# Two weighing steps in a row: pairs of column-tiled matmuls in units 1, 2, 9 and 10

## The chip, the core and the metric

The kernel is one program on one core of a Trainium2 chip. The metric is the device time of the launch in microseconds. A core has five engines that run side by side, each through its own queue and strictly in that queue's order: TensorE (PE, with its weight loads shown apart as PEld), VectorE (DVE), ScalarE (ACT), GpSimd (POOL) and SyncE (SP, which here issues DMAs). They wait for each other by semaphores.

## The reference

Four sequences of 512 tokens, 128 channels wide, go through three layers: a block of attention with rotary positions and a mixture of experts, a plain attention, and the first block again.

```python
def _L0_ffn_ref(src, ...):
    q = (src @ Wq).reshape(Bb, Tt, H, DH).transpose(0, 2, 1, 3)          # 16 heads of 8
    k = (src @ Wk_c @ Wk).reshape(Bb, Tt, H, DH).transpose(0, 2, 1, 3)
    v = (src @ Wv_c @ Wv).reshape(Bb, Tt, H, DH).transpose(0, 2, 1, 3)
    q, k = _apply_rope(q, sin, cos), _apply_rope(k, sin, cos)
    attn = jax.nn.softmax(jnp.einsum('bhqd,bhkd->bhqk', q, k) / np.sqrt(DH), axis=-1)
    sa = jnp.einsum('bhqk,bhkd->bhqd', attn, v).transpose(0, 2, 1, 3).reshape(Bb, Tt, C) @ Wo
    x = _rmsnorm(src + sa, norm1_w)
    shared = _swiglu(flat @ W_shared_in) @ W_shared_out
    ...                                   # a gate picks 2 of 8 experts, weights w
    h = _swiglu(flat @ W1_shared)
    for e in range(E):
        routed = routed + h @ W2_experts[e] * w[:, e:e + 1]
    return _rmsnorm(x + (shared + routed).reshape(Bb, Tt, C), norm2_w)

x = x + 0.5 * _L0_ffn_ref(_layernorm(x), ...)
x = x + _L0_attn_ref(_layernorm(x), ...)                                  # 16 heads of 4
x = x + 0.5 * _L0_ffn_ref(_layernorm(x), ...)
```

## The kernel before, in words

A unit is one sequence in one layer: units 0 to 3 and 8 to 11 are of the block with experts, 4 to 7 of the plain attention. What a unit does is cut into named steps, and `plan()` writes all steps of all units into one list. Each engine walks the same list and does its own share of each step. So the list is the order of the work on every engine.

The list is built from places. A unit has 64 places, and in each stands one tile of scores that goes into the softmax (`exp_scores`: a 128x512 matmul of keys and queries, L953, and the exponential of it by ACT, L1379, into `probs`). Beside it stands, as a rule, one tile of scores of the next unit whose row maxima are taken (`max_scores`: a matmul, L920, and a reduction on DVE, L1174). The maxima are made ready on POOL, turned on PE (`max_rows`, L927), copied by ACT (L1371) and sent by SP into the rows that the next unit's exponentials need.

Four tiles of exponentials are one step s of a unit's 16. `weigh_v` (L980) multiplies them with v: four matmuls of 18 columns each, in four column groups of the array that run at the same time, in f32, so 8 passes in the trace. `probs` has two buffers (`P_RING = 2`), step s uses buffer s % 2. So ACT's first exponential of step s waits until step s-2 has been weighed (the semaphore `out_done`), and `weigh_v` waits for the four exponentials of its step. It is put at `WEIGH_LATE = 2` places behind the last of them. After steps 7 and 15 ACT copies the sums out (`heads_evacuate`, L1391). In the last unit a weighing (L969) is cut otherwise: two parts of 256 columns, so 16 passes in a row.

All other steps stand at places in tables: `PREP_u` for what prepares unit u (two units ahead, beside unit u-2), `POST_u` for what follows unit u's attention (beside unit u+1): `heads_out`, `heads_transpose`, `out_project`, then `rms_stats` (ACT squares, L1410, then POOL, L1507 and L1511), `rms_apply1` (DVE, L1204), `x1_transpose` (PE, L1024, then a copy by ACT), `logits`, `mlp_up`, `router`, `shared_out` and `expert`, the second `rms_stats` and so on. Within a place exponentials come first, then maxima, then a weighing, then the steps of the tables.

Scores and most other products go through seven banks of PSUM. `Banks.take` gives a step the bank that its own bookkeeping (`HOLD`, tenths of a place) says is free longest; a matmul then waits until the former user's reader has released it.

Of the kernel before, what the change touches and what calls it, by code (L numbers as in the profile page):

```python
# [45 lines left out]
COL = 32  # L46
# [10 lines left out]
P_RING = 2  # L57
PIECES = 4
# [74 lines left out]
def exp_run(u):  # L133

    return 2 if u in EXP_PAIRS else 1

# [54 lines left out]
class Banks:  # L191
# [10 lines left out]
    def take(self, name, u, place, args):  # L202
# [14 lines left out]
        for i, _, _, then in uses:  # L217
# [24 lines left out]
PREP_10 = {"norm_stats": [-7], "norm_apply": [-1], "x_transpose": [17], "qk_project": [23, 36], "qk_split": [36, 37],  # L242
           "v_project": [19], "stack": [37, 72]}
PREP_11 = {"norm_stats": [8], "norm_apply": [11], "x_transpose": [16], "qk_project": [17, 50], "qk_split": [36, 55],
           "v_project": [31], "stack": [43, 74]}
# [20 lines left out]
POST_8 = {"heads_out": [3, 3], "heads_transpose": [6], "out_project": [10], "rms_stats": [11, 73],  # L266
          "rms_apply1": [15], "x1_transpose": [17], "logits": [19], "mlp_up": [28, 34, 34, 37],
          "router": [25, 27, 28, 30, 32, 36, 37, 50], "shared_out": [48], "expert": [50, 51, 55, 57, 60, 63, 66, 66],
          "rms_apply2": [76], "ffn_out": [97]}
POST_9 = {"heads_out": [2, 3], "heads_transpose": [7], "out_project": [9], "rms_stats": [13, 68], "rms_apply1": [16],  # L270
          "x1_transpose": [19], "logits": [21], "mlp_up": [21, 29, 29, 33],
          "router": [21, 21, 36, 37, 38, 40, 43, 43], "shared_out": [40], "expert": [44, 46, 52, 54, 54, 59, 59, 62],
          "rms_apply2": [73], "ffn_out": [85]}
POST_10 = {"heads_out": [3, 4], "heads_transpose": [6], "out_project": [8], "rms_stats": [9, 59], "rms_apply1": [15],
           "x1_transpose": [16], "logits": [24], "mlp_up": [17, 20, 31, 31],
           "router": [24, 28, 29, 29, 29, 29, 31, 32], "shared_out": [28],
           "expert": [34, 34, 40, 42, 42, 44, 46, 48], "rms_apply2": [61], "ffn_out": [75]}
# [8 lines left out]
MAX_LATE = [39, 33, 23, 18, 10, 18, 22, 24, 24, 17, 17, 13, 14]  # L286
# [70 lines left out]
def plan():  # L357
# [8 lines left out]
    for i in range(UNITS * TILES):  # L366
        if i % exp_run(i // TILES) == 0:
            put(together(i), "exp_scores", i // TILES, i % TILES // 4, i % 4)
# [40 lines left out]
def macaron(nc, x, w, out):  # L409

    steps = plan()
    with ExitStack() as ctx:
# [421 lines left out]
        def _(pe):  # L834
# [21 lines left out]
            for name, u, args, use in steps:  # L856
# [98 lines left out]
                elif name == "weigh_v":  # L955
# [3 lines left out]
                    if s == 0:  # L959
                        taken(pe, "v_project", u)  # L960
# [680 lines left out]
```

## Time and profile before

| | us |
|---|---|
| median of 3 runs | 836.71 (835.49 to 836.86) |
| the profiled execution's own time | 837.1 |
| span of its trace | 835.0 |
| PE busy in the span | 807.6 (97%) |
| DVE busy | 669.5 (80%) |
| ACT busy | 502.4 (60%) |
| POOL busy | 350.9 (42%) |

The span runs from the first to the last recorded instruction; 2.1 us of the execution lie outside it. A matmul's recorded time is its way through the array: matmuls follow each other more closely than they last, so the distance from start to start is what one costs. A weight load (PEld) normally lies under the matmul before it. Idle time of an engine is printed in brackets before an instruction, with what ended it.

### The profile page before, as it was taken

Reading aid. Unit: us, or ns where it says so; the run is one execution under the profiler, and the core shown is the slowest. Engines: PE = TensorE matmul, PEld = TensorE weight load, DVE = VectorE, ACT = ScalarE, POOL = GpSimd, SP = SyncE. Lnnn points to the kernel's source line nnn. Section 1 sums busy time; section 2 is a strip of 40 time slices with the busy share of each in tenths; the row PEclk is TensorE's granted clock in tenths of the full one; section 3 lists DMA queues with packets and bytes.
Section 4 is the critical chain, followed back from the end, with each engine's and each line's share of the span. In section 5 each row is a group of like instructions: output and inputs, shape, how many; then the busy total and the mean of one; then the engine's idle time right before and its main releaser. Section 6 shows DMA issues by size and latency. Waiting matters only on the chain.

```text
span 835.0 us, 13433 instructions
## 1 busy us (share of the span) xinstructions
PE 807.6 (97%) x4423; PEld 309.3 (37%) x4423; DVE 669.5 (80%) x1318; ACT 502.4 (60%) x1073; POOL 350.9 (42%) x746
## 2 busy tenths in 40 slices
PE   9799999999999999999999999999999999999995
PEld 4323344334333343332323232233433434355553
DVE  6899997697789758787989999988988687673266
ACT  3267664475467637755877777677764475375541
POOL 2564327714342353534442357334153623443532
PEclk9799999999999999999999999999999999999998
DMA  3452502110200010020010323204002200000000
GB/s 115 131 146 69 151 12 67 30 59 9 72 2 2 20 57 6 9 75 2 4 50 33 78 81 82 77 10 113 35 20 59 77 2 14 1 16 1 1 14 13
DMA packets 24699, 37.82 MB, mean 45 GB/s; under 512 B 6464, under 2 KB 22080, under 8 KB 23048
## 3 DMA queue, kind: packets, MB, share of 16 engines
q1 hardware_dynamic: 24053, 35.95, 15.2%
q10 hardware_dynamic: 579, 1.03, 0.4%
q8 instruction: 35, 0.57, 0.3%
q14 instruction: 32, 0.26, 0.1%
HBM read 27.03 MB, written 9.11 MB: 43 GB/s over the span
## 4 chain that ended last, share of the span: by engine, by line
PE 78%; DVE 12%; POOL 4%; issue 3%; ACT 1%; DMA 1%; SPq 0%; POOLq 0%; ACTq 0%; DVEq 0%
PE ps_out L980 16%; PE ps L920 14%; PE ps L953 13%; PE ps L1054 13%; DVE maxes L1174 8%; PE ps L1039 7%; PE ps L876 2%; PE ps_out L969 2%; PE ps L1046 2%; PE ps L941 2%; PE ps L886 1%; PE ps L1017 1%; DMA k_aug<-ones_row 1%; PE ps L1030 1%; PE ps L1005 1%
## 5 line engine op out<-in xcount | busy, mean ns | idle before, releaser
L1379 ACT ACTIVATE probs<-ps 128x512 f32<-128x512 f32 x768 | 414.4, 597 | 226.3 <-PE ps L953 204.8
L1174 DVE TENSOR_REDUCE maxes<-ps 128x1 f32<-128x512 f32 x768 | 479.5, 682 | 48.7 <-PE ps L920 46.6
L920 PE MATMUL ps<-k_aug,q_aug 72*128 72x512 bf16 (+1 forms) x768 | 246.8, 385 | 5.8 <-issue 4.0
L953 PE MATMUL ps<-q_aug,k_aug 75*128 75x512 bf16 (+1 forms) x704 | 231.5, 383 | 2.3 <-DVE maxes L1174 0.7
L980 PE MATMUL ps_out<-probs,v_aug 128*18 128x512 f32 x1408 | 185.4, 598 | 1.7 <-ACT probs L1379 1.0
L920 PEld LDWEIGHTS ps<-k_aug,q_aug 72*128 72x128 bf16 (+1 forms) x768 | 64.7, 97 | 166.6 <-issue 114.0
L1054 PE MATMUL ps<-w,hidden 128*128 128x512 f32 x256 | 118.8, 596 | 0.0
L953 PEld LDWEIGHTS ps<-q_aug,k_aug 75*128 75x128 bf16 (+1 forms) x704 | 58.9, 96 | 134.9 <-issue 88.7
L1271 DVE TENSOR_TENSOR prod<-ps,gate 128x512 f32<-128x512 f32 x56 | 38.7, 691 | 51.6 <-PE ps L1054 40.1
L1491 POOL TENSOR_SCALAR max_parts<-maxes 128x16 bf16<-128x16 f32 (+1 forms) x38 | 11.0, 289 | 144.1 <-DVE maxes L1174 143.8
L1571 POOL TENSOR_TENSOR prod<-prod 128x512 f32<-128x512 f32 x28 | 35.5, 1269 | 82.9 <-DVE prod L1271 70.2
L1054 PEld LDWEIGHTS ps<-w,hidden 128*128 128x128 f32 x256 | 47.0, 190 | 44.0 <-issue 40.8
L1039 PE MATMUL ps<-x1T,w_in 128*128 128x512 f32 (+1 forms) x144 | 60.5, 552 | 0.0
L980 PEld LDWEIGHTS ps_out<-probs,v_aug 128*18 128x18 f32 x1408 | 23.6, 96 | 66.6 <-issue 34.0
L1233 DVE SCALAR_TENSOR_TENSOR hidden<-hidden,ps 128x512 f32<-128x512 f32 (+1 forms) x36 | 22.6, 629 | 27.6 <-ACT hidden L1434 27.5
L1434 ACT ACTIVATE hidden<-ps 128x512 f32<-128x512 f32 (+1 forms) x36 | 19.8, 551 | 25.0 <-PE ps L1039 24.9
L1039 PEld LDWEIGHTS ps<-x1T,w_in 128*128 128x128 f32 x144 | 26.1, 190 | 20.0 <-issue 18.2
L670 POOL TENSOR_TENSOR rope_s<-rope_s,sinT 128x512 f32<-128x512 f32 x14 | 17.7, 1267 | 16.6 <-DVE rope_s L1156 16.6
L1238 DVE SCALAR_TENSOR_TENSOR hidden<-hidden,ps 128x512 f32<-128x512 f32 (+1 forms) x36 | 22.6, 628 | 1.2
L1466 POOL TENSOR_SCALAR var_eps<-mean_var 128x4 f32<-128x4 f32 x12 | 2.8, 230 | 49.1 <-DVE mean_var L1104 48.8
L1507 POOL TENSOR_SCALAR rms_in<-squared 128x4 f32<-128x4 f32 (+1 forms) x16 | 3.4, 210 | 44.4 <-ACT squares L1410 44.2
L704 POOL TENSOR_TENSOR parts<-rope_c,parts 128x512 bf16<-128x512 f32 x18 | 20.8, 1157 | 1.7
(160 smaller groups left out, 774.7 us busy)
## 6 DMA issues: line engine op xcount, KB each, us to landing
q_aug<-qk_parts SPq DMA_DIRECT2D x7, 1152.0 KB
k_aug<-qk_parts SPq DMA_DIRECT2D x21, 384.0 KB
qk_parts<-parts SPq DMA_DIRECT2D x48, 128.0 KB, 2.3
q_aug<-qk_parts SPq DMA_DIRECT2D x11, 288.0 KB
k_aug<-qk_parts SPq DMA_DIRECT2D x24, 96.0 KB
qk_parts<-parts SPq DMA_DIRECT2D x24, 64.0 KB, 2.0
X<-in_x_dram SPq DMA_DIRECT2D x4, 256.0 KB, 4.3
w<-in_ffn_W_experts_dram SPq DMA_DIRECT2D x2, 512.0 KB, 7.1
```

Of the source, the lines that this page charges most:

```text
L704: eng.tensor_tensor(l, rest, m, ALU.subtract).then_inc(done, two)
L920: pe.matmul(bank(use[i]), q_aug[p0:p1, r, at, qt * 128:(qt + 1) * 128], k_aug[p0:p1, r, at, :], start=True, stop=True).then_inc(bank_full[ ...
L953: pe.matmul(bank(use[i]), k_aug[p0:p1, r, at, kt * 128:(kt + 1) * 128], q_aug[p0:p1, r, at, :], start=True, stop=True).then_inc(bank_full[ ...
L980: mm = pe.matmul(ps_out[COL * c:COL * c + 2 * VW, :], v_aug[:, r, kt, 4 * (g // 2) + c, x0:x0 + 2 * VW], probs[:, n % P_RING, c, :], start ...
L1039: pe.matmul(bank(use[i])[:, cols], w_in[:, c // 2, c0:c0 + 128], x1T[:, cols], start=True, stop=True)\
L1054: mm = pe.matmul(o, hidden[:, 2 + k, t * 128:(t + 1) * 128], w2[:, k, half * EPG:(half + 1) * EPG, :].rearrange("p e n -> p (e n)"), start ...
L1174: dve.tensor_reduce(maxes[:, u % 2, qt, at:at + 1], full(use[0]), AX.X, ALU.max).then_inc(bank_free[use[0][0]], 1)
L1233: ins = dve.scalar_tensor_tensor(out=hidden[:, c, cols], in0=hidden[:, c, cols], scalar=1.0, in1=full(use[0])[:, cols], op0=ALU.add, op1=A ...
L1238: ins = dve.scalar_tensor_tensor(out=hidden[:, c, cols], in0=hidden[:, c, cols], scalar=0.5, in1=full(use[1])[:, cols], op0=ALU.mult, op1= ...
L1271: dve.tensor_tensor(prod[:, n % 2, half, :, :], o, gate[:, t, half * EPG:(half + 1) * EPG].unsqueeze(2) .to_broadcast([128, EPG, C]), ALU. ...
L1379: act.activation(probs[:, step % P_RING, c:c + exp_run(u), :], both(use), ACT.Exp, scale=scale)\
L1571: seq(pool.tensor_tensor(p[:, 0, :, :], p[:, 0, :, :], p[:, 1, :, :], ALU.add))
```

## The change

`DOUBLE_UNITS` names units 1, 2, 9 and 10. There `weigh_v` is put once for two steps: it waits for the last exponential of the second and then does the eight matmuls of both, from one buffer and then the other. The eight exponentials of such a pair are put into the first 6 of its 8 places (two each at the first and the fourth), and the weighing stands 3 places behind the last of them, which is the first place of the next pair, behind that place's two exponentials and one maximum. Each step still counts `out_done` by itself.

The tables of `PREP_10`, `PREP_11` and `POST_8` to `POST_10` (work beside units 8 to 11) have other places, and so have two entries of `MAX_LATE` and eight of `HOLD`, which changes which bank many tiles go to in all units. The tables beside units 1 and 2, except for bank choice, are as before. The same instructions are issued on every engine, in another order.

```diff
+DOUBLE_UNITS = {1, 2, 9, 10}
+DOUBLE_PACE = 6
+DOUBLE_LATE = 3
...
+def steps_at_once(u):
+
+    return 2 if u in DOUBLE_UNITS else 1
...
-POST_8 = {"heads_out": [3, 3], "heads_transpose": [6], "out_project": [10], "rms_stats": [11, 73],
+POST_8 = {"heads_out": [3, 3], "heads_transpose": [7], "out_project": [10], "rms_stats": [12, 69],
...
-MAX_LATE = [39, 33, 23, 18, 10, 18, 22, 24, 24, 17, 17, 13, 14]
+MAX_LATE = [39, 33, 23, 18, 11, 18, 22, 24, 24, 17, 15, 13, 14]
...
         if i % exp_run(i // TILES) == 0:
-            put(together(i), "exp_scores", i // TILES, i % TILES // 4, i % 4)
+            at = i - i % 8 + i % 8 * DOUBLE_PACE // 8 if i // TILES in DOUBLE_UNITS else i
+            put(together(at), "exp_scores", i // TILES, i % TILES // 4, i % 4)
...
-        for s in range(TILES // 4):
+        for s in range(steps_at_once(u) - 1, TILES // 4, steps_at_once(u)):
             late = u * TILES + 4 * s + 3 + WEIGH_LATE
+            if u in DOUBLE_UNITS:
+                late = u * TILES + 4 * s - 4 + 7 * DOUBLE_PACE // 8 + DOUBLE_LATE
             put(late, "weigh_v", u, s)
...
                 elif name == "weigh_v":
-                    s, = args
-                    g, kt, n = s // TT, s % TT, u * 16 + s
-                    taken(pe, "exp_scores", u, s, 4 - exp_run(u))
-                    if s == 0:
+                    last, = args
+                    taken(pe, "exp_scores", u, last, 4 - exp_run(u))
+                    if last == steps_at_once(u) - 1:
                         taken(pe, "v_project", u)
+                    for s in range(last - steps_at_once(u) + 1, last + 1):
+                        n = u * 16 + s
...
+                            for c in range(4):
+                                x0 = VW * (g % 2)
+                                mm = pe.matmul(ps_out[COL * c:COL * c + 2 * VW, :],
+                                               v_aug[:, r, kt, 4 * (g // 2) + c, x0:x0 + 2 * VW],
+                                               probs[:, n % P_RING, c, :], start=first_one, stop=last_one)
                         mm.then_inc(out_done, 1)
```

PE in unit 1, from the fourth step's weighing to the transpose of x1 (L1024), before. L953 is a tile for the exponentials, L920 one for the maxima, L980 a weighing, L865 the transpose of the unit being prepared.

```order
L980 MATMUL ps_out<-probs,v_aug 18x512 x4
L953 MATMUL ps<-q_aug,k_aug 128x512
L920 MATMUL ps<-k_aug,q_aug 128x512
L953 MATMUL ps<-q_aug,k_aug 128x512
L920 MATMUL ps<-k_aug,q_aug 128x512
L865 MATMUL ps<-ident,src 128x128 x4
L953 MATMUL ps<-q_aug,k_aug 128x512
L920 MATMUL ps<-k_aug,q_aug 128x512
L953 MATMUL ps<-q_aug,k_aug 128x512
L920 MATMUL ps<-k_aug,q_aug 128x512
L980 MATMUL ps_out<-probs,v_aug 18x512 x4
L1024 MATMUL ps<-ident,src 128x128 x4
```

The same place in the changed kernel, directly behind the double weighing of steps 2 and 3 (L964 is the exponentials' tile there, L931 the maxima's, L876 and L1037 the two transposes).

```order
L964 MATMUL ps<-q_aug,k_aug 128x512
L931 MATMUL ps<-k_aug,q_aug 128x512 x2
L964 MATMUL ps<-q_aug,k_aug 128x512
L931 MATMUL ps<-k_aug,q_aug 128x512
L964 MATMUL ps<-q_aug,k_aug 128x512 x2
L931 MATMUL ps<-k_aug,q_aug 128x512
L876 MATMUL ps<-ident,src 128x128 x4
L964 MATMUL ps<-q_aug,k_aug 128x512
L931 MATMUL ps<-k_aug,q_aug 128x512
L964 MATMUL ps<-q_aug,k_aug 128x512
L931 MATMUL ps<-k_aug,q_aug 128x512
L1037 MATMUL ps<-ident,src 128x128 x4
```

Between the two transposes there is no weighing any more, and the one between the squares and x1's transpose has moved ahead of the squares.

ACT near the end of unit 2 before: L1371 copies the maxima's rows, L1410 are the second squares of unit 1's post-processing, L1391 the copy of unit 2's second half of sums.

```order
L1371 ACTIVATE maxT<-ps 96x128
L1379 ACTIVATE probs<-ps 128x512 x9
L1410 ACTIVATE squares,squared<-src 128x128 x4
L1379 ACTIVATE probs<-ps 128x512 x6
L1391 ACTIVATE heads<-ps_out 128x512
```

The same in the changed kernel, its lines numbered 13 higher (L1392 is the exponential).

```order
L1384 ACTIVATE maxT<-ps 96x128
L1392 ACTIVATE probs<-ps 128x512 x10
L1423 ACTIVATE squares,squared<-src 128x128 x4
L1392 ACTIVATE probs<-ps 128x512 x3
L1404 ACTIVATE heads<-ps_out 128x512
```

The squares now stand between the sixth and the seventh exponential of the unit's last pair, and the weighing of both steps waits behind the eighth.

## Rows read from the trace of the kernel before

**Rows 1.** The page, busy time of the engines; the row of line 980

```profile
PE 807.6 (97%) x4423; PEld 309.3 (37%) x4423; DVE 669.5 (80%) x1318; ACT 502.4 (60%) x1073; POOL 350.9 (42%) x746
...
L980 PE MATMUL ps_out<-probs,v_aug 128*18 128x512 f32 x1408 | 185.4, 598 | 1.7 <-ACT probs L1379 1.0
```

**Rows 2.** Windows: units 1, 2, 6, 9, 10; length, each engine's busy, clock

```profile
99.70:176.90 77.20, 76.58 (x379) 30.64 (x378) 63.73 (x122) 42.91 (x95) 38.67 (x79) 1.00 0.19 56
176.90:252.80 75.90, 75.90 (x378) 30.49 (x377) 61.45 (x111) 42.94 (x95) 27.86 (x64) 1.00 0.07 23
440.70:486.70 46.00, 43.83 (x295) 12.26 (x293) 43.38 (x76) 36.39 (x74) 18.17 (x33) 1.00 0.19 52
589.20:665.00 75.80, 75.70 (x375) 30.32 (x374) 61.31 (x117) 41.94 (x87) 33.15 (x68) 1.00 0.15 43
665.00:737.60 72.60, 72.32 (x367) 28.78 (x370) 55.80 (x100) 41.97 (x97) 28.66 (x74) 1.00 0.02 5
```

**Rows 3.** Timeline, PE around a weighing: start, length in us

```profile
242.01 0.38 PE L920 MATMUL ps<-k_aug,q_aug 72*128 72x512 bf16 x1
...
242.23 0.38 PE L953 MATMUL ps<-q_aug,k_aug 75*128 75x512 bf16 x1
242.53 0.13 PEld L980 LDWEIGHTS ps_out<-probs,v_aug 128*18 128x18 f32 x8 [0.43 <-ACT probs L1379]
242.54 1.05 PE L980 MATMUL ps_out<-probs,v_aug 128*18 128x512 f32 x8
...
243.52 0.39 PE L920 MATMUL ps<-k_aug,q_aug 72*128 72x512 bf16 x1
```

**Rows 4.** Timeline, a weighing of the last unit, matmuls and weight loads

```profile
737.56 1.06 PE L969 MATMUL ps_out<-probs,v_aug 128*18 128x256 f32 x16
738.55 0.39 PE L941 MATMUL ps<-q_aug,k_aug 75*128 75x256 bf16 x2
...
737.56 0.57 PEld L969 LDWEIGHTS ps_out<-probs,v_aug 128*18 128x18 f32 x16 [0.32 <-issue]
```

**Rows 5.** Timeline, end of unit 2: ACT, and the last weighing

```profile
245.19 0.31 ACT L1410 ACTIVATE squares<-src 128x128 bf16<-128x128 f32 x1
...
246.37 3.00 ACT L1379 ACTIVATE probs<-ps 128x512 f32<-128x512 f32 x6
...
248.46 1.05 PE L980 MATMUL ps_out<-probs,v_aug 128*18 128x512 f32 x8
...
249.58 0.60 ACT L1391 ACTIVATE heads<-ps_out 128x512 f32<-128x512 f32 x1 [0.20 <-PE ps_out L980]
```

**Rows 6.** Timeline, unit 1, from the squares to x1's transpose

```profile
110.14 0.32 ACT L1410 ACTIVATE squares<-src 128x128 bf16<-128x128 f32 x1
...
111.77 1.04 POOL L1511 TENSOR_TENSOR rms<-rms_in,power 128x4 f32<-128x4 f32 x1
...
113.41 1.13 DVE L1204 SCALAR_TENSOR_TENSOR src<-src,rms,n 128x128 f32<-128x128 f32 x4
...
113.60 1.05 PE L980 MATMUL ps_out<-probs,v_aug 128*18 128x512 f32 x8
...
114.59 0.66 PE L1024 MATMUL ps<-ident,src 128*128 128x128 f32 x4
```

**Rows 7.** Line 1379, what ended ACT's idle time before it

```profile
PE ps L953: 204.8, 219
```

**Rows 8.** Timeline, start of unit 2: DVE and PE

```profile
174.79 0.39 PE L953 MATMUL ps<-q_aug,k_aug 75*128 75x512 bf16 x1 [0.48 <-DVE maxes L1174]
...
174.07 3.05 DVE L1174 TENSOR_REDUCE maxes<-ps 128x1 f32<-128x512 f32 x5
```

**Rows 9.** Unit 2's first maxima: DMA, first exponential's matmul; another DMA's landing

```profile
166.78 0.78 SPq L804 DMA_DIRECT2D q_aug<-maxT  x1
...
171.31 0.38 PE L953 MATMUL ps<-q_aug,k_aug 75*128 75x512 bf16 x1
...
qk_parts<-parts SPq DMA_DIRECT2D x48, 128.0 KB, 2.3
```

More of the change, by code:

```diff
@@ L241 @@
           "v_project": [24], "stack": [38, 67]}
[L242 to L245, printed above, removed]
+PREP_10 = {"norm_stats": [-8], "norm_apply": [-5], "x_transpose": [15], "qk_project": [20, 36], "qk_split": [42, 46],
+           "v_project": [20], "stack": [49, 72]}
+PREP_11 = {"norm_stats": [8], "norm_apply": [11], "x_transpose": [15], "qk_project": [19, 45], "qk_split": [33, 49],
+           "v_project": [29], "stack": [39, 59]}
 POST_0 = {"heads_out": [1, 1], "heads_transpose": [8], "out_project": [10], "rms_stats": [16, 53],
@@ L333, in post_steps @@
     return steps + stats[1:] + [(at["rms_apply2"][0], ("rms_apply2", u)), (at["ffn_out"][0], ("unit_out", u))]
-HOLD = {"x_transpose": 32, "qk_project": 31, "v_project": 32, "heads_transpose": 23, "out_project": 32,
-        "x1_transpose": 32, "logits": 32, "shared_out": 38, "expert": 33, "max_rows": 26, "heads_out": 27,
-        "mlp_up": 31, "replicate": 67, "max_scores": 28, "exp_scores": 22}
+HOLD = {"x_transpose": 32, "qk_project": 31, "v_project": 26, "heads_transpose": 23, "out_project": 35,
+        "x1_transpose": 26, "logits": 26, "shared_out": 38, "expert": 33, "max_rows": 23, "heads_out": 24,
+        "mlp_up": 25, "replicate": 61, "max_scores": 28, "exp_scores": 22}
 SEVERAL_BANKS = {"mlp_up": 2}
@@ L962, in _ @@
-                    if u == LAST:
-                        g, k2 = s // 2 % 4, s % 2
-                        if s % 4 == 0:
-                            pe.wait_ge(heads_done, 2 * u + s // 4)
-                        for i, c in itertools.product(range(2), range(4)):
-                            x0 = VW * (g % 2)
-                            mm = pe.matmul(ps_out[COL * c:COL * c + 2 * VW, 0:256],
-                                           v_aug[:, r, 2 * k2 + i, 4 * (g // 2) + c, x0:x0 + 2 * VW],
-                                           probs[:, n % P_RING, c, i * 256:(i + 1) * 256],
-                                           start=(s % 4 == 0 and i == 0), stop=(s % 4 == 3 and i == 1))
-                        mm.then_inc(out_done, 1)
-                        continue
```

45 lines of the change are left out of this document (26 added, 19 removed).

## The prediction

> **What bounds the kernel now.** I read the page first: PE is busy for 807.6 of 835.0 us, DVE for 80% and ACT for 60% [rows 1]. A share over the span says little, so next the windows by unit. In units 1, 2, 9 and 10, the four that change, PE is busy for 76.58 of 77.20, 75.90 of 75.90, 75.70 of 75.80 and 72.32 of 72.60 us, at a granted clock of 1.00, DVE for 77 to 83% and ACT for 55 to 58% [rows 2]. Unit 6 is of the other sort: PE leaves 2.2 of 46.0 us idle and DVE is at 94%. So in the four changed units what PE saves is saved, as long as nobody else is late; unit 6 and its neighbours gain nothing.
>
> Then the timeline around one weighing, for what it costs beyond its own columns [rows 3]. Start to start, two neighbouring tiles of scores are 0.22 us apart (242.01 to 242.23). From the last tile to the weighing it is 0.31 us (242.23 to 242.54), so 0.09 us more. From the weighing to the next tile it is 0.98 us here and 0.99 at others. Its 8 passes are two groups of four column groups. The page's row of line 980 gives a pass 0.598 us [rows 1]; 1.05 us for all eight puts the last pass 0.45 us behind the first, and from there to the next tile are 0.53 us, where a next group would have followed after about 0.43. What is left, some 0.13 us (0.99 less two groups at 0.43), is the way out of the column-tiled mode. One weighing thus pays about 0.09 us going in and 0.13 us coming out.
>
> **What the change removes.** 64 weighings become 32 pairs. If the second step follows the first like one more pair of groups, each pair pays the way in and out once instead of twice: 0.22 us less. 32 x 0.22 = 7.0 us. A pair then takes 4 x 0.43 + 0.13 = 1.85 us to the next tile. That steps can follow like this, with other weights, is what the last unit shows: 16 passes in four groups of 256 columns, with new weights in the third group, take 1.06 us and let the next tile start at 738.55, 0.99 us after the first [rows 4]. The 8 passes of 512 columns take the same 0.99, so two more groups and a change of weights in between cost nothing there.
>
> The Trainium skill, "TensorE: Matmul & The Clock Gate", section "Part 3: Packing small matmuls — row/col tiling", says something that speaks against this: weight loads overlap with running matmuls only where the row group differs. The column groups share all rows. By that rule the second step's loads would stand in the open, and the time would be the 838.8 of rival D below. This trace disagrees: the 16 loads of rows 4 spread over 0.57 us under the matmuls.
>
> **What it adds: ACT starts a pair later.** Before, ACT never waits for a weighing before an exponential. Its idle time there ends with a matmul of scores, 204.8 us in 219 waits, and no weighing is named [rows 7]. Now the first two exponentials of the next pair are issued in front of the weighing and need the buffer that its first step reads. A weighing lasts 1.05 us, and ACT follows 0.07 us behind the end (248.46 + 1.05 = 249.51, ACT at 249.58) [rows 5]. So with T0 as the weighing's start, ACT's queue stands until T0 + 1.12, everything behind those exponentials included. Exponentials back to back come every 0.48 us (6 in 3.00 us, the last 0.60 long) [rows 5]; eight end at 1.12 + 7 x 0.48 + 0.60 = T0 + 5.1. In a pair without other work PE comes to the next weighing at 1.85 + 15 x 0.22 + 0.31 = T0 + 5.4 to 5.5. So a bare pair is covered, with 0.3 to 0.4 us to spare, and ACT's other work is what can break it. I walked the pairs with the order of the changed kernel and these durations. The places that come out late:
>
> Unit 1, x1. Before, squares start at 110.14, POOL ends its part at 112.81 (111.77 + 1.04), DVE at 113.41 to 114.54, and x1's transpose at 114.59 comes exactly when PE is through with the weighing of 113.60 [rows 6]. There is no slack. Now the squares stand behind the double weighing and its two held exponentials: start at 1.12 + 2 x 0.48 = T0 + 2.1. The chain takes 4.40 us, of which 0.6 is DVE's queue (112.81 to 113.41); with half of that x1 is ready at T0 + 6.2. PE reaches the transpose at 1.85 + 12 x 0.22 + 0.44 = T0 + 4.9. It waits 1.3 us, and some 0.3 more for ACT's copy in front of the logits: 1.6 us.
>
> Unit 2, last pair. Squares take ACT 1.18 us (245.19 to 246.37) [rows 5]. They now stand in front of the seventh of eight exponentials. The sixth starts at about T0 + 4.1, the squares at 4.5, the last two exponentials end at 6.8, the weighing was due at 5.4: 1.4 us. Before, the same squares cost nothing, because six places lay between them and the next dependent weighing.
>
> Unit 2, second pair, and unit 9, second pair: squares in front of the eighth exponential. In unit 2 the projection stands late and the exponential ends at about 7.4 against PE at 6.7: 0.7 us. In unit 9 7.2 against 6.7: 0.5 us.
>
> Unit 10, x1: squares at T0 + 6.0, x1 at 10.4, PE at 9.8: 0.5 us. Its other pairs come out even.
>
> Start of unit 2: PE already waits 0.48 us for a bank that DVE has not read, since DVE is at a maximum every 0.61 us there (5 in 3.05) [rows 8]. Time that PE saves just before is not kept: 0.3 us.
>
> Sum of what comes back: 1.6 + 1.4 + 0.7 + 0.5 + 0.5 + 0.3 = 5.0 us. Bounds for it: nothing, if ACT and DVE run ahead as they do now; and 11 us, if in addition every second one of some 48 copies that ACT makes for PE in these four units (x, v, attention, x1, rows of maxima, the two halves of sums) falls into the 1.12 us hold and costs a quarter of a microsecond.
>
> **What it moves at no cost.** The exponentials' tiles stand up to 2 places earlier; they need banks, and two banks are held until ACT is released at T0 + 1.12. PE is in the weighing until 1.85, so they are free again before it asks; if bank choice puts a maximum behind them, that costs up to the 0.6 us of one exponential. The DMA with unit 2's first maxima is issued at 166.78, the first exponential that needs it at 171.31, 4.5 us later [rows 9]. Behind a double weighing I get some 2.4 us; a DMA of another kind lands after 2.3. I take nothing and keep 0.5 us as the bad end. SP's and POOL's orders hardly change. The other banks (`HOLD`) touch units 3 to 8, where PE waits for DVE's and ACT's speed and not for the choice of bank: nothing, at most 1 us either way. The moved table entries beside units 9 and 10 are in the walk above; beside unit 11 they reorder work of a busy PE: nothing.
>
> **The sum.** The profiled execution took 837.1 us. 837.1 - 7.0 + 5.0 = 835.1. It lies 0.4 us above the median of 836.71, so I take 834.7.
>
> **The rivals.** About 0.2%, 1.7 us, is what a measurement of this kernel can tell from no change.
>
> A. Nearly all is kept. For it: PE is at 100% in these units while ACT has over 40% left, and my walk puts late what a slightly idler DVE would do sooner (x1 ready 0.3 us earlier, POOL free). Against: the chain of rows 6 has no slack. 7.0 less 2 us: time 829.7 to 832.2.
>
> B. My forecast, 2.5 to 6.5 us of stalls: 832.2 to 836.2.
>
> C. It becomes slower: ACT's hold. The mechanism is the one above, at more places: every copy that PE waits for and that is queued behind the two held exponentials comes up to 1.1 us later, 8 times a unit. For it: no such wait exists now, and the tables of units 1 and 2 keep their places although the order changed under them. Against: PE has 30 us of other work in each of these units, mostly between the places that wait. It decides from 0.22 us lost per pair; at the upper bound, 11 us, the time is 840.7, at 9 us 838.7.
>
> D. The pair does not close up: the array empties between the two steps too, or the second step's eight weight loads, 0.13 us [rows 3], stand in the open. In the second case a pair saves 0.22 - 0.13 = 0.09 us and the kernel 2.9; in the first it saves nothing. Against the same 5.0 of stalls the time is 838.8 to 841.7. Rows 4 speak against both. The rule of the Trainium skill named above is the second case.
>
> E. The stalls cancel the gain within 1.7 us either way; this lies between B and C, 836.2 to 838.4.
>
> **How the numbers follow.** A 0.20, B 0.43, E 0.17, C 0.15, D 0.05. Faster by over 0.2% (below 835.0): A and 0.31 of B's 0.43, 0.51. Within 0.2% (835.0 to 838.4): the rest of B and all of E, 0.29. Slower: C and D, 0.20. The range from 830.8 to 839.5 leaves out the lower part of A (0.09) and the upper parts of C and D (0.10). B by itself is 832.2 to 836.2.
>
> **What would show it.** Right: weighings of 16 passes, the next tile 1.85 us behind their start, and the last pass of the first step 0.45 us behind its first, with the second step's first pass at 0.87. ACT's waits get a new row, an exponential that waits for `ps_out`, about 28 times. PE's idle time in unit 1 shows L1037 waiting for DVE by over 1 us, and in unit 2 a weighing that waits for ACT by over 1 us. Of its 1.76 us of savings unit 1 keeps about 0.2, unit 2 gives back all and 0.6 more, units 9 and 10 keep 1.3 each. Wrong: the next tile later than 1.95 us (then D), PE at 100% in all four units (then A), or waits at L1024, L1017 and L865's successors in most pairs (then C). If units 4 to 7 move by more than 1 us, the bank choice matters and I have left it out.

## The result, and the profile after

| | before | after |
|---|---|---|
| median of 3 runs, us | 836.71 (835.49 to 836.86) | 849.68 (846.35 to 851.1) |
| the profiled execution's own time | 837.1 | 849.68 |
| span of its trace | 835.0 | 847.9 |
| granted clock over the span | 0.991 | 0.98 |

The ratio is 1.0146 (1.0123 to 1.0169): slower by 12 to 13 us, outside the range of the prediction. The page's rows of the changed kernel that answer to [rows 1], with the clock's row (tenths of full speed in 40 slices) between:

```profile
PE 811.7 (96%) x4422; PEld 314.1 (37%) x4423; DVE 668.9 (79%) x1318; ACT 500.9 (59%) x1073; POOL 350.5 (41%) x746
...
PEclk9699999999999999999999999999999979999999
...
L992 PE MATMUL ps_out<-probs,v_aug 128*18 128x512 f32 x1408 | 183.6, 611 | 2.6 <-ACT probs L1392 2.0
```

PE's share of the span hardly moves, but slice 33 shows a clock of 0.7. The windows show where. The first four are units 1, 2, 9 and 10 as in [rows 2] (length, then each engine's busy time, then the granted clock), the last three are stretches inside units 1, 2 and 10:

```profile
101.30:183.90 82.60, 79.63 (x387) 31.89 (x388) 64.97 (x126) 42.74 (x95) 38.68 (x79) 0.98 0.16 48
183.90:261.40 77.50, 74.62 (x365) 30.33 (x364) 58.03 (x105) 41.15 (x91) 27.88 (x64) 0.98 0.07 22
601.10:675.50 74.40, 73.81 (x377) 31.73 (x380) 59.69 (x115) 41.07 (x90) 35.17 (x71) 1.00 0.17 44
675.50:750.10 74.60, 72.89 (x356) 30.74 (x358) 54.29 (x94) 40.04 (x95) 26.44 (x70) 0.93 0.02 5
117.30:120.70 3.40, 3.40 (x16) 0.64 (x19) 0.78 (x3) 0.46 (x1) 2.10 (x10) 0.50 0.00 0
253.80:257.20 3.40, 3.12 (x16) 0.51 (x16) 2.17 (x6) 0.82 (x2) 1.81 (x2) 0.50 0.00 0
687.30:697.50 10.20, 10.20 (x38) 4.30 (x39) 4.66 (x9) 2.77 (x5) 1.24 (x6) 0.50 0.09 25
```

PE now leaves 3.0 us of unit 1 idle (before 0.6), 2.9 of unit 2 (0.0) and 1.7 of unit 10 (0.3), and 17.0 us of the span that were at 2.4 GHz before run at 1.2 GHz. At the start of the program the stretch at 1.2 GHz is 13.7 us instead of 3.4 and 6.8. Unit 9 is the one that won: 74.40 against 75.80 us.

The timeline of PE in unit 1 (start, length) shows the saving itself:

```profile
108.60 0.39 PE L931 MATMUL ps<-k_aug,q_aug 72*128 72x512 bf16 x1
108.92 1.91 PE L992 MATMUL ps_out<-probs,v_aug 128*18 128x512 f32 x16
110.76 0.39 PE L964 MATMUL ps<-q_aug,k_aug 75*128 75x512 bf16 x1
...
112.82 0.39 PE L931 MATMUL ps<-k_aug,q_aug 72*128 72x512 bf16 x1 [0.36 <-ACT probs L1392]
...
115.04 0.66 PE L1037 MATMUL ps<-ident,src 128*128 128x128 f32 x4 [0.37 <-DVE src L1217]
```

Sixteen passes start at 108.92 and the next tile at 110.76, 1.84 us later; over the pairs of the trace it is 1.845, and the second step's first pass stands 0.87 us behind the first step's. The prediction had 1.85 and 0.87. The same lines hold the price: a tile of maxima waits for a bank that ACT still reads, and x1's transpose waits for DVE.

The waits behind it in units 2 and 10, on PE:

```profile
182.42 0.66 PE L1024 MATMUL ps<-ident,attn 128*128 128x128 f32 x4 [1.11 <-DVE attn L1203]
...
190.71 0.65 PE L876 MATMUL ps<-ident,src 128*128 128x128 f32 x4 [1.10 <-DVE src L1126]
...
251.99 0.82 PE L931 MATMUL ps<-k_aug,q_aug 72*128 72x512 bf16 x3 [0.18 <-DVE maxes L1187]
...
254.08 3.44 PE L992 MATMUL ps_out<-probs,v_aug 128*18 128x512 f32 x16 [1.03 <-ACT probs L1392]
257.46 0.39 PE L931 MATMUL ps<-k_aug,q_aug 72*128 72x512 bf16 x1
...
685.23 0.38 PE L931 MATMUL ps<-k_aug,q_aug 72*128 72x512 bf16 x1
687.24 1.09 PE L1037 MATMUL ps<-ident,src 128*128 128x128 f32 x4 [1.63 <-DVE src L1217]
688.12 0.63 PE L964 MATMUL ps<-q_aug,k_aug 75*128 75x512 bf16 x1
```

The first of them lies at the end of unit 1 as the windows cut it. Four idle waits of over 1 us, none of which the kernel before has (it has one of 1.03 us elsewhere, at 407.5, and so have all the others, without a fall of the clock). The last pair of unit 2 takes 3.38 us to the next tile instead of 1.84, since it runs at 1.2 GHz, and after the wait of 1.63 a tile of scores lasts 0.63 instead of 0.38.

**The books.** For them I took each distance from one matmul's start to the next in both traces and subtracted what the same neighbours cost without a wait at 2.4 GHz. The span grew by 12.9 us: 7.0 saved by the pairs, 10.0 more of waits at full clock (unit 1: 5.5 against 1.6; unit 2: 4.8 against 1.1; the rest in units 4, 9 and 10), and 9.9 more for passes at 1.2 GHz. The last agrees with the stretches, where work that runs at 1.2 GHz takes twice its time: half of 17.0 is 8.5, half of the 3.5 more at the start is 1.7, 10.2 together. The part at the start is not shown to come from the change: there the traces of the sixteen kernels have between 6.8 and 17.1 us at 1.2 GHz, and x1_filled, which starts with the same instructions as the changed kernel, has 6.8.

### The profile page after: what moved, and what is told of

Same layout as the page of the kernel before. It is cut to its first block, busy times and chain, and to the rows that moved or that the text cites. A ratio compares the mean times of both kernels' runs of the same rounds, so it can differ in the third digit from the quotient of the medians.

```text
span 847.9 us, 13433 instructions
## 1 busy us (share of the span) xinstructions
PE 811.7 (96%) x4422; PEld 314.1 (37%) x4423; DVE 668.9 (79%) x1318; ACT 500.9 (59%) x1073; POOL 350.5 (41%) x746
## 3 DMA queue, kind: packets, MB, share of 16 engines
q10 hardware_dynamic: 579, 1.03, 0.3%
## 4 chain that ended last, share of the span: by engine, by line
PE 75%; DVE 15%; issue 4%; POOL 4%; ACT 2%; DMA 0%; POOLq 0%; ACTq 0%; DVEq 0%
PE ps_out L992 16%; PE ps L931 13%; PE ps L1067 12%; PE ps L964 12%; DVE maxes L1187 9%; PE ps L1052 7%; PE ps L887 2%; PE ps L1059 2%; PE ps_out L980 2%; PE ps L952 2%; ACT probs L1392 1%; PE ps L897 1%; PE ps L1030 1%; PE ps L1043 1%; DVE src L1291 1%
## 5 line engine op out<-in xcount | busy, mean ns | idle before, releaser
L1392 ACT ACTIVATE probs<-ps 128x512 f32<-128x512 f32 x768 | 413.5, 598 | 247.5 <-PE ps L964 151.6
L931 PE MATMUL ps<-k_aug,q_aug 72*128 72x512 bf16 (+1 forms) x768 | 242.7, 387 | 7.4 <-issue 2.5
L964 PE MATMUL ps<-q_aug,k_aug 75*128 75x512 bf16 (+1 forms) x704 | 223.4, 385 | 2.1 <-DVE maxes L1187 0.4
L931 PEld LDWEIGHTS ps<-k_aug,q_aug 72*128 72x128 bf16 (+1 forms) x768 | 64.7, 98 | 158.0 <-issue 99.5
L964 PEld LDWEIGHTS ps<-q_aug,k_aug 75*128 75x128 bf16 (+1 forms) x704 | 58.8, 97 | 136.0 <-issue 87.8
L992 PEld LDWEIGHTS ps_out<-probs,v_aug 128*18 128x18 f32 x1408 | 27.3, 97 | 76.2 <-issue 53.3
L1052 PEld LDWEIGHTS ps<-x1T,w_in 128*128 128x128 f32 x144 | 26.0, 190 | 18.6 <-issue 14.9
```

What stands on the lines that cost most here:

```text
L931: pe.matmul(bank(use[i]), q_aug[p0:p1, r, at, qt * 128:(qt + 1) * 128], k_aug[p0:p1, r, at, :], start=True, stop=True).then_inc(bank_full[ ...
L964: pe.matmul(bank(use[i]), k_aug[p0:p1, r, at, kt * 128:(kt + 1) * 128], q_aug[p0:p1, r, at, :], start=True, stop=True).then_inc(bank_full[ ...
L992: mm = pe.matmul(ps_out[COL * c:COL * c + 2 * VW, :], v_aug[:, r, kt, 4 * (g // 2) + c, x0:x0 + 2 * VW], probs[:, n % P_RING, c, :], start ...
L1052: pe.matmul(bank(use[i])[:, cols], w_in[:, c // 2, c0:c0 + 128], x1T[:, cols], start=True, stop=True)\
L1392: act.activation(probs[:, step % P_RING, c:c + exp_run(u), :], both(use), ACT.Exp, scale=scale)\
```

## The experiments

All ratios are to the kernel before, from the same chip. A table first; each kernel then has its part.

| kernel | median us (range) | ratio (95%) |
|---|---|---|
| tables_alone | 841.07 (840.82 to 842.42) | 1.0055 (1.0040 to 1.0070) |
| pairs_old_tables | 842.90 (839.75 to 843.03) | 1.0074 (1.0057 to 1.0091) |
| three_buffers | 849.93 (846.66 to 851.70) | 1.0153 (1.0128 to 1.0178) |
| three_buffers_single | 836.43 (835.61 to 839.04) | 1.0000 (0.9991 to 1.0009) |
| steps_later | 845.74 (845.28 to 847.17) | 1.0114 (1.0099 to 1.0129) |
| x1_filled | 843.94 (841.72 to 845.67) | 1.0088 (1.0068 to 1.0108) |
| pairs_9_10 | 836.78 (835.62 to 837.39) | 1.0001 (0.9991 to 1.0010) |
| hold_alone | 840.16 (839.98 to 843.25) | 1.0053 (1.0033 to 1.0072) |
| old_hold | 849.64 (844.40 to 850.32) | 1.0144 (1.0120 to 1.0168) |
| x1_early | 837.80 (836.66 to 839.40) | 1.0014 (1.0005 to 1.0023) |
| x1_early_filled | 838.85 (838.48 to 839.29) | 1.0028 (1.0017 to 1.0040) |
| pairs_9_10_held | 843.12 (840.46 to 844.39) | 1.0072 (1.0058 to 1.0085) |
| waits_filled | 843.81 (841.84 to 844.91) | 1.0087 (1.0074 to 1.0100) |
| x1_earlier | 842.19 (840.68 to 847.30) | 1.0074 (1.0054 to 1.0094) |

**tables_alone and pairs_old_tables: which half of the change?**

```diff
-DOUBLE_UNITS = {1, 2, 9, 10}
+DOUBLE_UNITS = set()
```

> The changed kernel with no unit doubled: the new places in five tables, MAX_LATE and HOLD alone. My theory is that the loss of 13 us comes from the pairs (PE waits for ACT's late exponentials and for x1, and TensorE's clock falls to its lower level behind such waits); then this is within 2 us of before, 835 to 839. Rival: the moved tables and the other banks cost it; then 845 or more.

The second keeps the pairs and takes `PREP_10`, `PREP_11`, `POST_8` to `POST_10`, `MAX_LATE` and `HOLD` from the kernel before.

> The pairs in units 1, 2, 9 and 10, with before's tables, MAX_LATE and HOLD. My theory: 845 to 853, as slow as the changed kernel or slower, since units 9 and 10 lose what their tables gave. Rival (the tables and banks are the loss): 829 to 835.

By the ratios each half is slower by itself, by 4.6 and 6.2 us, and the two together by 12.2. In the trace of pairs_old_tables units 1 and 2 are 3.8 us longer, from first exponential to first exponential; since the pairs save 3.5 us there, the waits grew by 7.3. Between start and tail that trace has no stretch at 1.2 GHz. So the pairs as such lose, by their waits alone, and the tables do not make up for it.

In the trace of tables_alone unit 10 is the one that grew most, by 2.1 us. POOL, DVE and PE there:

```profile
680.85 1.26 POOL L1607 TENSOR_TENSOR X<-X,src 128x512 f32<-128x512 f32 x1
680.91 2.14 DVE L1217 SCALAR_TENSOR_TENSOR src<-src,rms,n 128x128 f32<-128x128 f32 x4 [0.85 <-POOL rms L1524]
683.10 0.66 PE L1037 MATMUL ps<-ident,src 128*128 128x128 f32 x4 [0.84 <-DVE src L1217]
```

The four products that make x1 take 2.14 us instead of 1.13 [rows 6], because POOL adds unit 8's result to `X` (L1607, 128x512) at the same moment. The moved tables put it there: `ffn_out` in `POST_8` stood at place 97 and now stands at 81, which is place 17 of unit 10. All six traces with the new tables have this one slow product (1.35 to 1.36 us), and none of the ten with the tables of before. No run moved this entry alone.

**three_buffers and three_buffers_single: is it ACT's hold (rival C)?** With three buffers the first exponentials of a pair need not wait for its predecessor's weighing. To make room, both kernels leave out half of the experts' second weights and the table of sines, and read the other half and the cosines in their place, with the same matmuls and products.

```diff
-P_RING = 2
+P_RING = 3
...
-        w2 = sb("w2", [128, 2, E, C])
+        w2 = sb("w2", [128, 1, E, C])
```

> The changed kernel with three buffers of probabilities, so that the next pair's first exponentials do not wait for the weighing. To make room, half of the experts' weights and the table of sines are left out (their places are read from the other half and the cosines). If ACT's hold of about 1.1 us per pair is what makes PE wait: below 840, no row in which an exponential waits for ps_out, and the clock stays up in units 1, 2, 9 and 10. If it is the order alone (squares in front of the last exponentials, the weighing gone between squares and x1's transpose): 845 or more.

> The kernel before with the same three buffers and the same parts left out, as the yardstick for the run with three buffers. No exponential waits for a weighing there, so both theories expect no change: 835 to 838.

What ended ACT's idle time in front of an exponential (total us, times, longest), first in the changed kernel, then with three buffers, and there the weighing at the end of unit 2:

```profile
ACT probs L1392 <- PE ps L964: 151.6, 183, 6.5
ACT probs L1392 <- PE ps_out L992: 73.1, 30, 5.2
```

```profile
ACT probs L1391 <- PE ps L963: 207.6, 205, 6.5
```

```profile
255.76 1.05 PE L991 MATMUL ps_out<-probs,v_aug 128*18 128x512 f32 x8 [1.03 <-ACT probs L1391]
```

The changed kernel has the 30 waits for `ps_out` that were forecast (28); with three buffers there is none, and yet the time is the same to 0.3 us and the wait of 1.03 us stands where it stood. ACT's hold costs nothing that these times show. What makes that weighing late is the order alone: four squares stand in front of the seventh exponential, and the weighing is due behind the eighth. Rival C is refuted in its mechanism.

**steps_later: can the waits be moved out of the way?** Four units in pairs, old tables, and each step that had waited is put one to four places later.

```diff
-          "rms_apply1": [19], "x1_transpose": [21], "logits": [23], "mlp_up": [24, 27, 27, 33],
+          "rms_apply1": [19], "x1_transpose": [24], "logits": [26], "mlp_up": [27, 29, 29, 34],
...
-POST_1 = {"heads_out": [4, 4], "heads_transpose": [6], "out_project": [11], "rms_stats": [12, 59],
+POST_1 = {"heads_out": [4, 4], "heads_transpose": [8], "out_project": [11], "rms_stats": [13, 61],
```

> The four pairs with before's tables, but the steps on which PE waited in the run with the old tables are put later: the transposes of attention (units 1, 8 and 9's) behind the double weighing at place 8, x for unit 4 behind the one at place 16, x1 of units 0 and 9 two or three places later, unit 1's squares behind the last exponential of a pair, unit 4's statistics four places later. If the loss is PE arriving early at steps whose chain through DVE or ACT has its old length, the waits of some 12 us in these units fall to 5 or less and the kernel takes 831 to 835, faster than before. Rival: pairs cost by themselves (banks, ACT's hold); then 840 or more.

It lost 2.8 us more than pairs_old_tables. Some of the waits did not vanish but went to the next in the queue. In unit 10, on PE:

```profile
683.22 0.39 PE L931 MATMUL ps<-k_aug,q_aug 72*128 72x512 bf16 x1 [0.88 <-DVE maxes L1187]
...
685.39 1.48 PE L1043 MATMUL ps<-w_gate,x1T 128*128 128x10 f32 x8 [0.31 <-ACT x1T L1437]
...
686.72 3.76 PE L1052 MATMUL ps<-x1T,w_in 128*128 128x512 f32 x4
```

PE, which saves 0.22 us per pair and has dropped the weighing that stood between, runs into the banks of the maxima, which DVE reads at 0.61 us each as in [rows 8]. And at 685.9 the clock falls again, for 6.8 us, after 3.4 at 180.7. By the distances between matmuls the waits of the four units together are as long as in pairs_old_tables to 0.5 us: 1.2 us fewer in unit 9, 1.5 more in unit 10. What is longer in the trace is mainly the 10.2 us at 1.2 GHz, where pairs_old_tables has none; they cost about 5 us of the 5.7 us between the spans (837.9 and 843.6). The theory that each wait is only a step placed too early found no support in this run.

**x1_filled: what does the fall of the clock cost?** In front of x1's transpose in units 1 and 10, which waits anyway, PE does 2 and 6 matmuls that nobody reads. No chain gets shorter by it.

```diff
-                    pe.wait_ge(x1_done, f + 1)
...
+                    for _ in range({0: 2, 9: 6}.get(u, 0)):
+                        pe.matmul(o, k_aug[0:72, (u + 1) % AUG_RING, 0, 0:128], q_aug[0:72, (u + 1) % AUG_RING, 0, :],
+                                  start=True, stop=True)
+                    pe.wait_ge(x1_done, f + 1)
```

> The changed kernel with 2 and 6 matmuls of 128x512 (nobody reads them) put in front of the transposes of x1 in units 1 and 10, where PE waited 0.5 and 1.8 us for DVE; the chains stay as long as they are. If the lower clock at 117 and 687 us came behind these waits, both stretches (3.4 and 10.2 us) disappear and the time falls by 5 to 7 us, to 842 to 845, though not one wait of the chain is shorter. If the clock falls for another reason: 848 to 851 and the stretches stay.

```profile
684.64 1.46 PE L1036 MATMUL ps<-q_aug,k_aug 72*128 72x512 bf16 x6
686.44 0.66 PE L1040 MATMUL ps<-ident,src 128*128 128x128 f32 x4 [0.34 <-DVE src L1220]
```

```profile
680.00:697.00 17.00, 16.66 (x91) 6.81 (x90) 14.27 (x27) 11.66 (x29) 6.54 (x20) 1.00 0.06 18
...
343.50:347.00 3.50, 3.50 (x15) 0.77 (x14) 2.06 (x4) 2.06 (x5) 1.37 (x5) 0.51 0.00 0
```

PE idles only 0.34 us between the last unread matmul and the transpose, and the window around it is at full clock: the 10.2 us at 1.2 GHz are gone, and unit 10 is 4.6 us shorter than in the changed kernel. The median gains 5.7 us of the 13. Two short stretches at 1.2 GHz remain, at 251.4 and, new, at 343.6 in a unit that the change does not touch.

**pairs_9_10: do the pairs pay where PE was at 100%?** Old tables, `DOUBLE_UNITS = {9, 10}`.

> Pairs in units 9 and 10 alone, before's tables and banks' bookkeeping. In the run with the old tables these two units came out 0.47 and 0.44 us shorter (1.76 saved by the pairs in each, the rest waited away) and unit 11 1.0 longer. Theory: 836 to 838, no change. Rival (pairs pay where the code around them does not change): 833 to 835.

No change: 16 pairs save 3.5 us, and the trace shows them waited away in some ten waits of 0.1 to 0.8 us by the distance between matmuls (0.5 us twice for DVE's attention, 0.8 and 0.3 for banks, the others smaller), no stretch at 1.2 GHz among them.

**hold_alone and old_hold: the bank choice.** The first is the kernel before with the eight changed entries of `HOLD`, the second the changed kernel with the old ones.

```diff
-HOLD = {"x_transpose": 32, "qk_project": 31, "v_project": 32, "heads_transpose": 23, "out_project": 32,
-        "x1_transpose": 32, "logits": 32, "shared_out": 38, "expert": 33, "max_rows": 26, "heads_out": 27,
-        "mlp_up": 31, "replicate": 67, "max_scores": 28, "exp_scores": 22}
+HOLD = {"x_transpose": 32, "qk_project": 31, "v_project": 26, "heads_transpose": 23, "out_project": 35,
+        "x1_transpose": 26, "logits": 26, "shared_out": 38, "expert": 33, "max_rows": 23, "heads_out": 24,
+        "mlp_up": 25, "replicate": 61, "max_scores": 28, "exp_scores": 22}
```

> The kernel before with the changed kernel's HOLD alone, so the same order and other banks. My prediction took the banks for free (1 us at most). The tables alone cost 4 us; if the banks have a part in it, this is 838 to 840 with the start and units 3 and 4 longer; if it is the places, 836 to 838.

> The changed kernel (pairs and new places) with before's HOLD, so before's bookkeeping of banks. HOLD alone cost 3.3 us on the kernel before, the pairs alone 6.1, and all together 12.9. If the parts add up: 844 to 847. If the banks only matter without the pairs: 848 to 851. Below 843 would say that banks and pairs together are worse than each.

Alone the entries cost 3.3 us by the medians and 4.4 by the ratio. In the trace unit 3 is 1.5 us longer (a tile of maxima waits 1.2 us for a bank behind DVE), unit 10 0.8, unit 4 0.6, and the start 1.0, where 13.7 us are at 1.2 GHz. In the changed kernel the old entries bring nothing that can be told from none (849.64 against 849.68, the four times of the first between 844.40 and 850.32). So their cost is not one term that adds. That PE's new waits cover it there is a guess.

**x1_early, x1_early_filled and x1_earlier: a wait by itself in the kernel before.** x1's transpose in unit 10 stands 2 or 3 places earlier, and nothing else changes; the filled one has 9 unread matmuls in the gap.

```diff
-           "x1_transpose": [19], "logits": [21], "mlp_up": [21, 29, 29, 33],
+           "x1_transpose": [17], "logits": [21], "mlp_up": [21, 29, 29, 33],
```

> The kernel before with unit 9's x1 transposed two places earlier (place 17 instead of 19 of unit 10), so that PE waits there once for some 2 us. No pairs. If a wait costs its own length and PE catches nothing up: 838.5 to 839.5. If TensorE's clock falls behind it, as it did in the changed kernel: 840 to 844, with a stretch at the lower level right behind 680 us.

> The same early x1, with nine unread matmuls of 128x512 (2.0 us) in front of it in place of the idle wait. Same chain, same length. If the clock is what makes the wait dear: the stretch at the lower level is gone and the time is 838 to 840, less than without the filling, or equal to it if the clock did not fall there. Rival (extra matmuls only add): as x1_early or up to 2 us more.

> The kernel before with unit 9's x1 transposed at place 16 instead of 19: one idle wait of about 2.5 us instead of 1.2 (place 17, which cost 1.0 us and no clock). If the clock falls behind a long enough wait alone, without a double weighing near it: 841 to 845 and a stretch at the lower level at about 676 us. If it needs the pair: 838.5 to 840, the wait's own length.

The transpose in x1_early, then in x1_earlier with its weighing behind it:

```profile
676.25 0.66 PE L1024 MATMUL ps<-ident,src 128*128 128x128 f32 x4 [1.03 <-DVE src L1204]
```

```profile
673.07 0.38 PE L920 MATMUL ps<-k_aug,q_aug 72*128 72x512 bf16 x1
...
676.51 1.11 PE L1024 MATMUL ps<-ident,src 128*128 128x128 f32 x4 [3.06 <-DVE src L1204]
...
678.09 1.91 PE L980 MATMUL ps_out<-probs,v_aug 128*18 128x512 f32 x8
```

```profile
664.00:671.00 7.00, 7.00 (x47) 3.04 (x48) 6.04 (x12) 5.60 (x17) 3.08 (x6) 1.00 0.00 0
671.00:678.00 7.00, 3.94 (x21) 1.60 (x13) 5.41 (x14) 3.51 (x14) 2.86 (x7) 0.78 0.00 0
678.00:682.00 4.00, 4.00 (x15) 0.89 (x14) 1.26 (x2) 1.71 (x5) 0.00 (x0) 0.50 0.05 10
```

One idle wait of 1.03 us costs 1.1 us in the trace and 1.0 in the median: its own length and no more, and the clock stays. Filled, it costs 2.1, for the nine matmuls overshoot the gap. One of 3.06 us in a PE that had been at 100% comes with 10.2 us at 1.2 GHz. They begin inside the wait, at about 675.0 (a clock of 0.78 over 671 to 678 is 3 us at half speed), and last 8.7 us beyond it, in which a weighing takes 1.91 us instead of 1.05; unit 10 becomes 6.5 us longer and the median 5.6. So in this pair of kernels the shorter wait costs its length and the longer one more than that.

**pairs_9_10_held and waits_filled: two attempts to keep the gain.** The first takes pairs_9_10, counts the banks of a pair's exponentials as held 1.5 places longer, and moves two transposes of attention later.

```diff
+            if name == "exp_scores" and u in DOUBLE_UNITS:
+                self.free_at[i] += 15
```

> Pairs in units 9 and 10 with before's tables, and two mendings: the bookkeeping counts an exponential's tile in these units as held 1.5 places longer, so that nobody is put behind a bank that ACT still holds (PE waited there 0.76, 0.31, 0.27 and three times 0.19 us), and heads_transpose behind the double weighing at place 8 (0.53 us twice). If these waits are where the 3.5 us of the pairs went: 834 to 835.5, faster than before. If pairs cost by themselves: 836.5 to 838.

It is 6.3 us slower than pairs_9_10: a tile of exponentials now waits 0.88 us for a bank whose maximum DVE has not taken, x1's transpose 0.74, and at 685.2 there are 3.4 us at 1.2 GHz. The second is the changed kernel with unread matmuls in front of four waits (x1's in units 1 and 10 as in x1_filled, five ahead of the transpose of unit 1's attention, five ahead of that of x for unit 4), and unit 1's second squares two places further on, with their `rms_apply2` one place.

```diff
+                    for _ in range({1: 5}.get(u, 0)):
...
+                    for _ in range({4: 5}.get(u, 0)):
...
-POST_1 = {"heads_out": [4, 4], "heads_transpose": [6], "out_project": [11], "rms_stats": [12, 59],
+POST_1 = {"heads_out": [4, 4], "heads_transpose": [6], "out_project": [11], "rms_stats": [12, 61],
```

> The changed kernel with unread matmuls in front of the four steps on which PE waited longest for DVE (2 and 6 before x1 in units 1 and 10, 5 before the transpose of attention and 5 before x for unit 4 in unit 2), and unit 1's second squares put behind the last exponentials. No chain is shorter. By the trace the 12.9 us are -7.0 for the pairs, +10.0 for waits and +9.9 for the clock at its lower level. If so, the stretches at the lower level between 45 and 830 us go and what is left is 837 - 7 + 9 = 839 to 841. If the clock falls by itself and not behind waits: 846 or more.

```profile
45.00:830.00 785.00, 767.95 (x4308) 296.80 (x4307) 626.54 (x1217) 485.55 (x1041) 332.44 (x711) 1.00 0.14 41
```

In the profiled execution (841.84 us) the clock is at full between start and tail: of the 12.9 us of span 7.9 are back. The median is 843.8. The other executions have a mean clock of 0.987 to 0.990 against 0.991, so part of the difference is likely to be further stretches at 1.2 GHz; no trace shows them. What is left above the kernel before are waits (and matmuls put into them). No kernel tried beats it.

## Why the prediction was wrong, step by step

**What one pair saves: right.** 7.0 us, from 1.845 us per pair, and the second step follows like one more pair of groups. Rival D (the pair does not close up) is refuted. The rule of the Trainium skill named in the prediction ("TensorE: Matmul & The Clock Gate", "Part 3: Packing small matmuls — row/col tiling") would have given 1.98 us to the next tile; this trace disagrees with it here too. The Trainium skill, "TensorEngine Tiling (Array Packing)", section "Key Properties", says that changing the tiling mode drains TensorE. This trace agrees: each pair is spared one change in and one out, and is 0.22 us shorter. The number type changes along with the mode, from bf16 to f32, and no run separates the two.

**The sum of the waits, 5.0 us: wrong, 10.0 measured.** The walk found the right kind of wait, and some in size: in unit 1 x1's transpose starts at T0 + 6.1 (forecast 6.2), and the waits from T0 to the logits come to 1.4 us (forecast 1.6), of which 0.5 is a tile of maxima that waits for a bank; at the end of unit 2 the weighing behind the squares 1.1 (1.4). What it missed are places where the late chain was not ACT's but DVE's. Beside unit 2 the transposes of attention and of x wait 1.3 us each with their start-up, and tiles of maxima at the end of unit 1 wait 1.1 together. The step that failed is "as long as nobody else is late" with a walk whose terms, but for the last, followed only ACT's queue from T0. Before, a weighing of 1.05 us stood on PE between many a step and the one that needs its result, and gave DVE the time; now it stands elsewhere, and DVE's queue, at 77 to 83% [rows 2] and one maximum per 0.61 us [rows 8], has no more slack than that. In unit 2, on PE and DVE:

```profile
179.40 1.04 PE L1018 MATMUL ps<-ident,heads 128*128 128x128 f32 x8
...
180.24 0.68 DVE L1187 TENSOR_REDUCE maxes<-ps 128x1 f32<-128x512 f32 x1
180.84 0.35 DVE L1197 RECIPROCAL denom<-ps 128x32 f32<-128x32 f32 x1
181.22 0.42 DVE L1203 TENSOR_TENSOR attn<-ps,denom 128x256 f32<-128x256 f32 x1
181.56 0.35 DVE L1197 RECIPROCAL denom<-ps 128x32 f32<-128x32 f32 x1
181.94 0.43 DVE L1203 TENSOR_TENSOR attn<-ps,denom 128x256 f32<-128x256 f32 x1
```

PE is through with the sums at 180.44, but DVE is in a maximum until 180.9 and needs 1.5 us from there, to 182.37. PE has four tiles of scores in the meantime, and is done with them at 181.31. Before, a weighing stood in this place, behind the sums of 175.47:

```profile
176.91 1.05 PE L980 MATMUL ps_out<-probs,v_aug 128*18 128x512 f32 x8
...
178.63 0.66 PE L1011 MATMUL ps<-ident,attn 128*128 128x128 f32 x4
```

The transpose of attention followed the end of the sums by 2.1 us then and by 2.0 us now. The chain is no longer than it was; the weighing, 0.98 us to the next tile, filled it, and now PE idles for 1.11. For the other waits behind DVE this reading was not tested by a run of its own.

**Unit 10's x1, 0.5 us: wrong, 1.8.** The chain of 4.40 us [rows 6] was carried over as a constant. Here it took 5.7 us, by POOL's queue and by a slower DVE. The squares start at T0 + 6.0, as forecast. On ACT, POOL and DVE:

```profile
681.47 0.33 ACT L1423 ACTIVATE squares<-src 128x128 bf16<-128x128 f32 x1
...
683.69 0.19 POOL L1520 TENSOR_SCALAR rms_in<-squared 128x4 f32<-128x4 f32 x1
683.97 1.04 POOL L1524 TENSOR_TENSOR rms<-rms_in,power 128x4 f32<-128x4 f32 x1
684.98 1.26 POOL L1607 TENSOR_TENSOR X<-X,src 128x512 f32<-128x512 f32 x1
...
685.04 2.14 DVE L1217 SCALAR_TENSOR_TENSOR src<-src,rms,n 128x128 f32<-128x128 f32 x4 [0.28 <-POOL rms L1524]
```

POOL splits maxima until 683.6, and the four products take DVE 2.14 us instead of 1.13. The second is the meeting with POOL's sum into `X` that tables_alone shows too. So the step "The moved table entries beside units 9 and 10 are in the walk above" failed as well: the walk had no term for POOL's sum, which the new tables put beside x1. It is 1.0 us of the wait of 1.63; without it an estimated 0.6 is left, close to the forecast of 0.5. Neither half by itself has this wait at this length: in pairs_old_tables PE idles for 0.25 us before x1 in unit 10, in tables_alone for 0.84.

**The clock: a term that was missing, 9.9 us.** The prediction read a granted clock of 1.00 in all four units and priced a wait at its length. That holds for the wait of 1.03 us in x1_early and not for 3.06 us in x1_earlier. In the changed kernel shorter waits are enough at times: the one of 1.63 us at 687 is followed by 10.2 us at 1.2 GHz, and 3.4 us begin during the one of 1.03 us at 254. For the first the cause is shown: in all three traces in which PE idles there for 1.6 us (this one, three_buffers, old_hold) a stretch of 6.8 or 10.2 us follows within 3 us, and in both in which the wait is filled (x1_filled, waits_filled) there is none.

The length of one wait does not tell, though. Between start and tail the traces of all kernels have twelve stretches at 1.2 GHz. Three come with those waits, one with that of 3.06 us, and two with the weighing at the end of unit 2, which waits 1.03 us in four traces (in three_buffers and old_hold without a fall). The other six have no wait of over 0.9 us in the 8 us before them: the stretch at 117.3 in the changed kernel comes behind waits of 0.36 and 0.37 us, that at 343.6 in x1_filled behind 0.46. And the ten waits of 1.1 us before the transposes of attention and of x, in five traces, have no fall behind them. With the waits' own 5.0 us beyond forecast the clock makes the miss: 5.0 + 9.9 = 14.9, against 834.7 for a profiled 849.7.

**The bank choice, "nothing, at most 1 us either way": wrong by itself, without effect here.** Alone it costs 3.3 to 4.4 us, in the changed kernel nothing measurable.

**ACT's hold (rival C), 0.15: the sign was right and the mechanism wrong.** Thirty waits for `ps_out`, and taking them all away changes nothing. Its upper end, 840.7, was too low as well, since it priced waits without the clock.

**By units** the prediction had -0.2, +0.6, -1.3, -1.3 for units 1, 2, 9 and 10. By the windows against [rows 2] they are +5.4, +1.6, -1.4 and +2.0, of which only unit 9 is right. Those windows begin with a unit's first weighing, which in a pair comes later, so up to a few us of the first belong to its neighbours; from first exponential to first exponential it is +3.1, +2.1, -2.2 and +4.4, and +3.9 for unit 3, into whose start unit 2's last weighing and its fall of the clock have moved.

**Open.** How much of the difference between medians is clock in the executions without a trace is not known; their mean clock (0.980 to 0.986 for the changed kernel) says it is of the size of the profiled one. What decides whether a wait is followed by a fall was not found. Which of the moved table entries cost what was not tested, the meeting of POOL and DVE in unit 10 included.

## What to carry to other kernels

Here a saving on the busiest engine was not kept, because the second had too little slack; where PE is at 100% and DVE at 80%, look at what the work covered before you take it from PE. Moving a long instruction away from between a step and its dependent removes cover of up to its full length, whatever it saves itself. When a table is moved, check every engine's queue at the new place: one entry put POOL's sum beside DVE's products. And price new idle waits of TensorE with the clock's possible fall, not only by their length, even when each is below a microsecond. If a long one cannot be avoided, matmuls that nobody reads, sized to end before the wait does, kept the clock here in both kernels that tried them.

## What the hardware showed that I had not expected

- One idle wait of 3.06 us in a TensorE busy at 100% before it comes with 10.2 us at 1.2 GHz, 8.7 of them behind it, and costs 5.6 us in all; one of 1.03 us costs 1.0. The Trainium skill, "TensorE: Matmul & The Clock Gate", section "A second HAM failure mode: psum-queue depth-cycling", tells of a kernel whose clock went back and forth because TensorE was idle for short moments between groups of matmuls. This case agrees: 3.4 to 10.2 us at 1.2 GHz beside waits of 0.4 to 1.6 us, but not beside each.
- Six matmuls that nobody reads, 1.46 us of work, gave back 4.6 us in unit 10.
- A product on DVE of 128x128 with two operands and a scalar takes 0.34 us; the one that met POOL's 128x512 sum took 1.35. The line's row:

```profile
L1217 DVE SCALAR_TENSOR_TENSOR src<-src,rms,n x32: 339/342/1352, 113.9 to 826.1; 128x128 f32<-128x128 f32 x32
```

  The Trainium skill, "GPSIMD Engine Reference", section "1. Specifications", says that GpSimd shares its interface to the memory with VectorE when that reads two operands from there. The traces agree for this meeting, which six of them have (1.35 to 1.36 us each); POOL's own 1.26 us is its usual length. They show no such loss beside POOL's short pieces of 0.2 to 0.4 us, where the product takes 0.34 to 0.37.
